# Sixteen groups of bins that end in two pairs, in place of fifteen that end in four threes

## The chip, the cores and the metric

The kernel runs on one core of a Trainium2 chip. The metric is the device time of one execution in microseconds. An execution under the profiler is slower than a timed one, and the two are kept apart below.

## The reference

A graph layer is followed by a mixture of eight experts, over 6,250 nodes with 256 features and 100,000 edges that are sorted by target:

```
x = x + GNN(layernorm(x)):  agg = segment_sum(xn[dst], src);  h = agg + xn
                            out = (h @ W1 + b1) @ W2 + b2
x = x + FFN(layernorm(x)):  for each of 8 experts: h1 = relu(bn(y @ W1)), h2 = relu(bn(h1 @ W2)), h2 @ Wo + bo
                            summed with the weights softmax(y @ Wr + br)
```

The sum over the edges is the sparse part. The experts are the dense part. Their matrices are 256x256, and each product is made as three half-precision passes (high x high, high x low, low x high).

## The kernel before

**Bins and entries.** The 6,250 nodes are 49 bins of 128. A prologue (the first 300 us of the profile) sorts the edges on the chip, makes the normalised and projected rows, writes them to memory (`xn_hilo`), and splits the weights. The edges then stand in 830 entries of up to 128 edges that all belong to one bin. 830 is fixed, as `BOUND`, whatever the edges are. GpSimd fetches each entry with one indirect DMA of 128 rows into `gbuf` (L544), a ring of 18 slots; before an even entry from the 18th on it waits until TensorE has used up the pair that held the slots. TensorE multiplies each entry by a one-hot matrix (L1504, L1505: two matmuls of 256 columns each, so four for a pair of entries). VectorE adds the result into the bin's row block `acc` (L1071) and makes the one-hot matrix of a later entry (L1002).

**Groups and steps.** The dense part goes through the bins in groups whose sizes are `GS`. A group of T bins takes eight steps, one for each expert. In step x TensorE issues, in this order:

- the first layer of step x+1, in two halves (L1, L1555): 6 matmuls each, 128\*T columns wide
- the third layer of step x-1 for the first two bins of the group (L3, L1589): 6 matmuls of 256 columns for each bin
- the second layer of step x, in two halves (L2, L1571), 6 matmuls each, 128\*T columns wide
- the third layer of step x-1 for bins three and four, if there are any

ScalarE makes, for each half of the first and the second layer, the rectified half-precision part (L730, L741) and the full one (L731, L742). VectorE subtracts the two to get the low part (L1167, L1173), and weighs the third layer into the output rows (L1190). The third layer of step x waits for the low parts of both halves of the second layer of step x.

**Where entries go.** `entry_plan` spreads the 415 pairs of entries over the steps. In steps 0 to 4 of group g the pairs that group g+1 needs are completed; from step 5 on the plan works for group g+2. The need of the first b bins is b/49 of the 830 entries. Thirteen pairs belong to the prologue. In a step the pairs stand at fixed places between the dense parts (`PLACES`). Entries and third layers share three PSUM banks in turn.

**Between groups.** In steps 3 to 7 of group g the next group's rows get their bias and aggregate, statistics, square root (L680), normalisation (L687), transposes (L1517), the logits of the router (L1527) and their exponentials (L716). SyncE loads a group's rows one group ahead and stores them when the last expert has been added (L459, L468).

Of the kernel before, what the change touches and what calls it, by code (L numbers as in the profile page):

```python
# [45 lines left out]
TILES = -(-E_EDGES // P)  # L46
BOUND = TILES + BINS - 1
GT = 4
GS = [1, 2, 3, 3] + [GT] * 7 + [3] * 4
G = len(GS)  # L50
FIRST = [sum(GS[:g]) for g in range(G + 1)]
NENT = BOUND
# [50 lines left out]
def nhalf(g):  # L103
    return 2 if GS[g] > 2 else 1

# [5 lines left out]
def bins_of(g, half):  # L111
    return range(2 * half, min(2 * half + 2, GS[g]))

# [30 lines left out]
def build(nc, x, src, dst, gW1, gb1, gW2, gb2, Wr, br, bn, W1, W2, Wo, bo, out):  # L144
    xn_dram = nc.dram_tensor("xn_hilo", (NPAD, 2 * D), F16, kind="Internal").ap()
    x_dram = nc.dram_tensor("x_whole_bins", (NPAD, D), F32, kind="Internal").ap()
    with ExitStack() as ctx:
# [160 lines left out]
        def loads_upto(g):  # L308

            return 16 * sum(GS[i] for i in range(g % 2, g + 1, 2))  # L310

# [84 lines left out]
        def _(sp):  # L396
# [56 lines left out]
            def load_x(g):  # L453
# [3 lines left out]
                    skip_runtime_bounds_check_because=IN_RANGE)  # L457
                for i in range(GS[g]):
                    sp.dma_start(xt[:, g % 2, i, :], x_dram[bass.ds(b[i] * P, P), :]).then_inc(s[f"xt_in{g % 2}"], 16)  # L459
# [1248 lines left out]
```

## Time and profile before

| | |
|---|---|
| timed runs | 1381.16, 1381.36, 1383.55 us, median 1381.36 |
| profiled execution | span 1595.0 us from the first to the last instruction; no other time of it is given |
| busy in the profile | PE 80%, VectorE 75%, ScalarE 54%, GpSimd 50% |
| mean granted TensorE clock | 0.928 of full speed |
| first and last indirect DMA issued | 235.8 and 1497.0 us |

The profiled execution takes 214 us more than a timed one. So a duration of a single instruction is taken from the profile, but the length of a stretch has to be looked through for idle time that the timed run may not have.

### The profile page before, as it was taken

To read this page: it belongs to the slowest core of one execution; us is meant where nothing else is said; L and a number is where in the kernel's file an instruction comes from. 1 tells how busy PE (TensorE), PEld (TensorE's weight loads), DVE (VectorE), ACT (ScalarE), POOL (GpSimd) and SP (SyncE) were. 2 spreads that over 40 slices of the span, in tenths; PEclk is the share of its full clock that TensorE was granted. 3 is DMA by queue.
4 is the path that set the end of the run, shared out by engine and by line. 5 is a ranking of instruction groups with operands and counts; after the bars stand their busy time and mean duration, and the time that the engine had idled before them with its cause. 6 is when DMAs were issued, how large, how long until landed. Compare 5 with 4: busy or idle time off the path is not lost.

```text
span 1595.0 us, 25908 instructions
## 1 busy us (share of the span) xinstructions
PE 1279.8 (80%) x8179; PEld 841.9 (53%) x8179; DVE 1197.4 (75%) x3476; ACT 868.3 (54%) x1623; POOL 805.0 (50%) x864
## 2 busy tenths in 40 slices
PE   3868885557687778888878878898888998788998
PEld 3746652345454445455545545554555666565665
DVE  9999985566667666777777877777778887777865
ACT  7887451344455435454445544555545665555685
POOL 3000006666556666666666666666666556656300
PEclk9969997778799988999999999999999999999999
DMA  9301135333232332333333333343333323332200
GB/s 292 99 0 53 54 100 170 109 98 103 83 103 86 110 91 87 111 88 100 102 89 113 87 90 113 87 116 87 89 111 88 107 83 107 88 105 86 74 11 11
DMA packets 82235, 150.86 MB, mean 95 GB/s; under 512 B 16855, under 2 KB 55034, under 8 KB 82100
## 3 DMA queue, kind: packets, MB, share of 16 engines
q0 software_dynamic: 39840, 108.84, 23.8%
q1 hardware_dynamic: 42260, 40.36, 8.0%
q8 instruction: 67, 1.10, 0.3%
q14 instruction: 68, 0.56, 0.1%
HBM read 129.87 MB, written 19.27 MB: 94 GB/s over the span
## 4 chain that ended last, share of the span: by engine, by line
PE 47%; DVE 24%; issue 12%; another core or an unknown queue 8%; ACT 7%; DVEq 2%; ACTq 0%
PE PA L1555 11%; PE PB L1571 11%; DVE acc L1071 5%; PE PL L1589 4%; DVE zz L837 4%; PE PT L1589 4%; PE PN L1589 3%; DVE zz L838 3%; DVE onehot L1002 2%; DVE xt L1190 2%; ACT PB L742 2%; PE PN L1505 2%; PE PT L1505 1%; PE PT L1504 1%
## 5 line engine op out<-in xcount | busy, mean ns | idle before, releaser
L544 POOL DMA_INDIRECT gbuf<-xn_hilo,dsti x830 | 790.3, 952 | 667.5 <-issue 196.8
L741 ACT ACTIVATE h<-PB,bnt,bns 128x512 f16<-128x512 f32 (+3 forms) x240 | 167.7, 699 | 325.9 <-remote 177.5
L1555 PE MATMUL PA<-yT,wsplit 128*128 128x512 f16 (+3 forms) x1440 | 318.1, 361 | 13.0 <-issue 9.4
L1571 PE MATMUL PB<-h,wsplit 128*128 128x512 f16 (+3 forms) x1440 | 300.3, 347 | 5.6 <-issue 5.6
L730 ACT ACTIVATE h<-PA,bnt,bns 128x512 f16<-128x512 f32 (+3 forms) x240 | 167.8, 699 | 215.8 <-remote 104.2
L1555 PEld LDWEIGHTS PA<-yT,wsplit 128*128 128x128 f16 x1440 | 143.3, 103 | 114.9 <-issue 31.3
L1173 DVE TENSOR_TENSOR h<-PB,h 128x512 f16<-128x512 f32 (+3 forms) x240 | 139.9, 587 | 84.8 <-ACT PB L742 64.5
L1571 PEld LDWEIGHTS PB<-h,wsplit 128*128 128x128 f16 x1440 | 141.2, 101 | 98.3 <-issue 13.0
L1002 DVE TENSOR_SCALAR onehot<-iota_row,srel 128x128 f16<-128x128 f16 x830 | 178.2, 267 | 0.0
L1167 DVE TENSOR_TENSOR h<-PA,h 128x512 f16<-128x512 f32 (+3 forms) x240 | 139.5, 587 | 40.2 <-ACT PA L731 31.8
L1071 DVE TENSOR_TENSOR acc<-acc,PN 128x256 f32 x276 | 114.0, 413 | 71.9 <-issue 23.8
L731 ACT ACTIVATE PA<-PA,bnt,bns 128x512 f32<-128x512 f32 (+3 forms) x240 | 160.8, 670 | 0.0
L742 ACT ACTIVATE PB<-PB,bnt,bns 128x512 f32<-128x512 f32 (+3 forms) x240 | 160.6, 669 | 0.0
L1071 DVE TENSOR_TENSOR acc<-acc,PT 128x256 f32 x286 | 118.0, 413 | 46.5 <-remote 16.1
L1071 DVE TENSOR_TENSOR acc<-acc,PL 128x256 f32 x268 | 110.6, 413 | 51.6 <-remote 21.1
L1589 PE MATMUL PN<-wsplit,h 128*128 128x256 f16 x792 | 104.9, 281 | 24.2 <-DVE xt L1190 7.2
L1589 PE MATMUL PL<-wsplit,h 128*128 128x256 f16 x828 | 107.6, 278 | 18.9 <-DVE acc L1071 6.3
L1589 PE MATMUL PT<-wsplit,h 128*128 128x256 f16 x732 | 96.1, 280 | 14.9 <-DVE acc L1071 7.2
L1589 PEld LDWEIGHTS PN<-wsplit,h 128*128 128x128 f16 x792 | 77.6, 100 | 50.1 <-issue 32.5
L1589 PEld LDWEIGHTS PL<-wsplit,h 128*128 128x128 f16 x828 | 80.1, 99 | 45.1 <-issue 24.7
L1504 PE MATMUL PN<-gbuf,onehot 128*128 128x256 f16 x276 | 72.2, 286 | 36.8 <-issue 28.8
L1504 PE MATMUL PL<-gbuf,onehot 128*128 128x256 f16 x268 | 70.7, 287 | 35.5 <-issue 30.6
(250 smaller groups left out, 1856.5 us busy)
## 6 DMA issues: line engine op xcount, KB each, us to landing
gbuf<-xn_hilo,dsti POOLq DMA_INDIRECT x830
xt<-x_whole_bins SPq DMA_DIRECT2D x49, 128.0 KB
out<-xt SPq DMA_DIRECT2D x49, 128.0 KB
acc<-in_x SPq DMA_DIRECT2D x4, 1536.0 KB
x_whole_bins<-acc SPq DMA_DIRECT2D x4, 1536.0 KB, 11.8
xn_hilo<-xt SPq DMA_DIRECT2D x24, 256.0 KB, 2.1
h<-in_L_ffn_W SPq DMA_DIRECT2D x9, 256.0 KB, 4.3
zz<-in_L_ffn_W SPq DMA_DIRECT2D x5, 256.0 KB
```

Source lines behind the costliest of these rows:

```text
L544: pool.indirect_dma_start(gbuf[:, k % SLOTS, :], None, xn_dram, bass.IndirectOffsetOnAxis(dsti[:, k:k + 1], 0)).then_inc(gat[k % SLOTS], 16)
L730: nc.scalar.activation(h1[:, e % 2, 0, h, 0:w], PA[:, h, 0:w], ACT.Relu, bias=sh, scale=sc)
L731: nc.scalar.activation(PA[:, h, 0:w], PA[:, h, 0:w], ACT.Relu, bias=sh, scale=sc).then_inc(s["z1_ready"], 1)
L741: nc.scalar.activation(h2[:, e % 2, 0, h, 0:w], PB[:, h, 0:w], ACT.Relu, bias=sh, scale=sc)
L742: nc.scalar.activation(PB[:, h, 0:w], PB[:, h, 0:w], ACT.Relu, bias=sh, scale=sc).then_inc(s["z2_ready"], 1)
L1002: ins = V.tensor_scalar(onehot[:, k % SLOTS, :], iota_row[:], srel[:, k:k + 1], None, ALU.is_equal)
L1071: V.tensor_tensor(to, to, bank(("E", p))[:, i, :], ALU.add).then_inc(s["acc_done"], 1)
L1173: V.tensor_tensor(h2[:, e % 2, 1, h, 0:w], PB[:, h, 0:w], h2[:, e % 2, 0, h, 0:w], ALU.subtract).then_inc(s["lo2_ready"], 1)
L1504: T_.matmul(to[:, i, :], onehot[:, m, :], gbuf[:, m, 0:D], start=True, stop=False)
L1555: last = T_.matmul(PA[:, h, 0:w], wsp[0][:, e, k, wp, h * P:(h + 1) * P], yT[:, g % 2, yp, k, 0:w], start=n == 0, stop=n == 5)
L1571: last = T_.matmul(PB[:, h, 0:w], wsp[1][:, e, k, wp, h * P:(h + 1) * P], h1[:, e % 2, yp, k, 0:w], start=n == 0, stop=n == 5)
L1589: last = T_.matmul(to[:, i % 2, :], h2[:, e % 2, yp, k, i * P:(i + 1) * P], wsp[2][:, e, k, wp, :], start=n == 0, stop=n == 5)
```

## The change

One line of sizes. A group of four goes, and the last of the four groups of three is followed by two groups of two:

```diff
-GS = [1, 2, 3, 3] + [GT] * 7 + [3] * 4
+GS = [1, 2, 3, 3] + [GT] * 6 + [3] * 4 + [2] * 2
```

Both lists sum to 49 bins. Everything else follows from `GS`: the number of groups, the widths of the matmuls and activations, the registers that address the bins, and the plan of the entries.

## Rows read from the trace of the kernel before

**Rows 1.** The page, engines: busy time, share of the span, instructions.

```profile
PE 1279.8 (80%) x8179; PEld 841.9 (53%) x8179; DVE 1197.4 (75%) x3476; ACT 868.3 (54%) x1623; POOL 805.0 (50%) x864
```

**Rows 2.** Windows, groups 0, 8, 10, 13, 14: length, busy PE PEld DVE ACT POOL, clock, DMA, GB/s.

```profile
301.10:373.00 71.90, 45.03 (x371) 34.25 (x370) 45.57 (x166) 34.43 (x85) 46.12 (x48) 0.80 0.37 108
...
1050.10:1152.90 102.80, 86.51 (x564) 51.69 (x565) 77.16 (x238) 52.06 (x83) 64.72 (x69) 0.98 0.34 98
...
1246.40:1327.00 80.60, 78.32 (x532) 50.37 (x529) 65.21 (x196) 50.14 (x80) 48.10 (x51) 0.98 0.32 94
...
1484.20:1544.00 59.80, 55.91 (x420) 38.89 (x418) 44.76 (x126) 43.74 (x80) 9.36 (x10) 1.00 0.13 36
1544.00:1595.00 51.00, 43.01 (x310) 29.54 (x307) 28.60 (x67) 32.64 (x57) 0.00 (x0) 0.98 0.05 16
```

**Rows 3.** Windows of line L742 alone: length, busy time and count, clock, DMA.

```profile
1050.10:1152.90 102.80, 11.94 (x16) 0.98 0.34 98
```

**Rows 4.** Waits of GpSimd: in total, times, longest.

```profile
POOL gbuf L544 <- issue: 196.8, 641, 0.7
```

**Rows 5.** Timeline of GpSimd, the first and the last gather: start, duration, idle before.

```profile
235.82 1.19 POOL L544 DMA_INDIRECT gbuf<-xn_hilo,dsti  x1 [195.71 <-DVE dsti L1012]
```

```profile
1496.96 0.94 POOL L544 DMA_INDIRECT gbuf<-xn_hilo,dsti  x1 [0.31 <-issue]
```

**Rows 6.** Timeline, a stall in group 12.

```profile
1444.18 0.67 ACT L741 ACTIVATE h<-PB,bnt,bns 128x384 f16<-128x384 f32 x1 [4.18 <-remote]
```

**Rows 7.** Timeline of PE in group 10, four bins: a half layer and what follows it.

```profile
1277.64 1.46 PE L1555 MATMUL PA<-yT,wsplit 128*128 128x512 f16 x6
1278.94 0.27 PE L1504 MATMUL PN<-gbuf,onehot 128*128 128x256 f16 x1
```

**Rows 8.** The chain of waits in group 14, one step: start, length, what.

```profile
1564.28 1.95 PE PA L1555 x12
1566.23 1.31 PE PT L1589 x12
1567.54 1.95 PE PB L1571 x12
1569.49 0.65 PE PN L1589 x6
```

**Rows 9.** Timeline of the last two steps of group 14, where no first layer is left.

```profile
1583.31 1.47 PE L1589 MATMUL PT<-wsplit,h 128*128 128x256 f16 x12 [1.43 <-ACT PB L742]
...
1584.61 2.11 PE L1571 MATMUL PB<-h,wsplit 128*128 128x384 f16 x12
...
1585.79 0.67 ACT L741 ACTIVATE h<-PB,bnt,bns 128x384 f16<-128x384 f32 x1 [3.17 <-PE PB L1571]
...
1586.92 0.67 ACT L741 ACTIVATE h<-PB,bnt,bns 128x384 f16<-128x384 f32 x1
...
1587.47 0.65 ACT L742 ACTIVATE PB<-PB,bnt,bns 128x384 f32<-128x384 f32 x1
1588.15 0.56 DVE L1173 TENSOR_TENSOR h<-PB,h 128x384 f16<-128x384 f32 x1 [0.57 <-ACT PB L742]
...
1588.81 1.47 PE L1589 MATMUL PL<-wsplit,h 128*128 128x256 f16 x12 [1.43 <-ACT PB L742]
```

**Rows 10.** Timeline of group 1, two bins: ScalarE and PE.

```profile
390.88 0.56 ACT L741 ACTIVATE h<-PB,bnt,bns 128x256 f16<-128x256 f32 x1 [5.36 <-remote]
391.34 0.53 ACT L742 ACTIVATE PB<-PB,bnt,bns 128x256 f32<-128x256 f32 x1
...
391.79 0.56 ACT L741 ACTIVATE h<-PB,bnt,bns 128x256 f16<-128x256 f32 x1
...
396.84 0.82 PE L1571 MATMUL PB<-h,wsplit 128*128 128x256 f16 x6
```

**Rows 11.** Groups by line and shape: count, busy us, mean ns, idle before.

```profile
L742 ACT ACTIVATE PB<-PB,bnt,bns 128x256 f32<-128x256 f32 x16 | 8.6, 537 | 0.0
...
L1173 DVE TENSOR_TENSOR h<-PB,h 128x256 f16<-128x256 f32 x16 | 6.4, 416 | 1.5 <-ACT PB L742 1.5
```

## The prediction

> **What bounds the kernel now.** I read the page first. TensorE is busy for 80% of the span, but no engine is full [rows 1], and the profiled span of 1595.0 us is 214 us over the timed 1381.4. So I cut the dense part into its fifteen groups. The cuts are where ScalarE begins the second layer of a group's first step; a group holds 16 instructions of L742 [rows 3]. Then I asked which resource each group's length follows [rows 2].
>
> Group 10 (four bins, 25 pairs of entries) takes 80.6 us with PE busy for 78.3 of it: it is bound by TensorE. Group 8 (four bins, 34 pairs) takes 102.8 us with PE busy for only 86.5, and holds 68 gathers (a 69th is cut by the border), which is 1.51 us for each. The gap comes from stalls in which ScalarE, VectorE and GpSimd all wait for results of TensorE that the trace shows as finished some us before [rows 6]. They come in nearly every group with gathers, and hardly in groups 10 and 14. I take them as the profiler's share, for this reason: a gather that waits for nothing is busy 0.95 us and then 0.31 us idle "issue" (196.8 us in 641 times) [rows 4], so 1.26 us. From the first gather at 235.8, 830 of them at 1.26 end at 1281.6; behind the last gather the profile has another 98.0 us, to 1595.0 [rows 5]. That makes 1379.6, against 1381.4 timed. So the timed run is at the pace of GpSimd's gathers almost to the end of the gathers, without the stalls.
>
> TensorE stands close behind. A half layer of 512 columns takes 1.30 us for 6 matmuls [rows 7], 0.217 each, a third layer 0.109 for each matmul of 256 columns [rows 8], so a pair of entries (four such) takes 0.44. Group 10 with 34 pairs in place of 25 would take 80.6 + 9 x 0.44 = 84.6 us of TensorE; its gathers would take 68 x 1.26 = 85.7. Four-bin groups in the middle are thus balanced, gathers ahead by one us. Group 13 (three bins, 15 pairs) takes 59.8 us, and group 14 (three bins, no entries) 51.0. A three-bin step in group 14 is TensorE alone: 1.95 + 1.31 + 1.95 + 0.65 = 5.86 us [rows 8].
>
> **The change, part by part.** The plan's arithmetic gives the pairs of each group. Groups 0 to 7 stay as they are. From there:
>
> - before, from group 8: 4 bins/34 pairs, 4/31, 4/25, 3/26, 3/25, 3/15, 3/0
> - after, from group 8: 4/31, 4/25, 3/26, 3/25, 3/22, 3/17, 2/10, 2/0
>
> So four groups are the same, only earlier. What goes is 4/34, 3/15 and 3/0. What comes is 3/22, 3/17, 2/10 and 2/0.
>
> *What goes.* 4/34: 85.7 us by its gathers (84.6 by TensorE; 102.8 as profiled, the far bound). 3/15: eight steps of 5.86 are 46.9, 15 pairs are 6.6, together 53.5; the group took 59.8, so 6.3 us belong to the work for the next group and to a stall of some 2 us. I take 5.5 for that work (bounds 4.4 and 6.3), so 59.0. 3/0: 51.0. In all 195.7 us.
>
> *3/22 and 3/17.* 46.9 + 22 x 0.44 + 5.5 = 62.1, and 46.9 + 17 x 0.44 + 5.5 = 59.9. Their gathers take 55.4 and 42.8 us, less than that, so they are hidden behind TensorE. This is 122.0 us.
>
> *A two-bin step.* TensorE's columns for a bin are the same in any group. The 6 matmuls of a half layer with 256 columns span 0.82 us with the last one's modelled 0.27 [rows 10], so 0.11 each: half the price of 512 columns. A step costs TensorE 36 x 0.109 = 3.93 us. The split costs the columns nothing. [...]
>
> But a two-bin step is too short for its own chain. The third layer of step x needs the low part of the second half of layer two, and stands ahead of layer two of step x+1 in TensorE's queue. The last steps of group 14 show this loop with nothing else in it [rows 9]: third layer at 1583.31, second layer at 1584.61 (1.30), ScalarE at 1585.79 (1.18), its second half at 1586.92 (1.13), the full part at 1587.47 (0.55), VectorE at 1588.15 (0.68), the next third layer at 1588.81 (0.66). The loop is 5.50 us, under TensorE's 5.86, so it costs nothing at three bins. At two bins: 1.31 for 12 matmuls as before; 6 x 0.109 + 0.2 = 0.86 to ScalarE; 0.91 for its half (390.88 to 391.79) and 0.46 to the full part [rows 10]; that takes 0.54, then 0.04 to VectorE; its subtraction 0.42 [rows 11] and 0.10 to TensorE. Sum 4.64 us, against TensorE's 3.93. ScalarE's load of four such halves is 3.65, so it is not the bound itself. Bounds for the step are 3.93 (the loop does not bind) and 5.2 (clock, below); I take 4.64, since every part has its row. With two pairs in a step TensorE has 3.93 + 0.87 = 4.80 and becomes the bound again; the entries fill the gap that the loop leaves.
>
> *2/10 and 2/0.* 2/10: five steps of 4.80, three of 4.64, and the work for the next group. That was 5.5 for three bins; most of it is in single instructions (table loads, square root, statistics) that do not shrink with the bins, so 4.5 (bounds 3 and 6): 42.4 us. 2/0: group 14 took 51.0, of which 46.9 are steps; its last two ran at 5.50, so 4.8 us stand outside; one bin less in the last third layer, weighing and store takes 0.9 off. 8 x 4.64 + 3.9 = 41.0. Together 83.4 us.
>
> *Edits at no cost.* SyncE's loads and stores stay 49 each; the load for the last group waits for a store of the group before, and has two steps (9 us) before its rows are wanted. GpSimd's 830 gathers are the same. Their ring gives a lead of at most nine pairs, which the last four-bin group, bound by TensorE, fills in both kernels.
>
> *Sum.* 122.0 + 83.4 - 195.7 = +9.7 us. On the timed median: 1391. A little of the lower clock that group 0 shows (0.80) can come back in groups with gaps in every step, so I say 1392.
>
> **The rivals.**
>
> *The loop does not bind (no change).* If layers one of later steps and the activations slip past each other so that a two-bin step costs 3.93, the eleven steps without entries save 0.71 each, 7.8 in all: +1.9 us, 1383. For it: group 14 runs without a gap at three bins. Against it: the loop of 5.50 is seen, and the order on TensorE is fixed. 14%.
>
> *The gathers bind to the end (faster).* What the kernel does after its last gather shrinks. Before, 98.0 us follow it. After, the last gather is let go when pair 406 is used up, in the first step of 2/10, and some 84 us follow. If the groups before ran at the gathers' pace the time would be 14 us less: 1367. In the profiled execution, at 1.51 us for each gather, 3/22 would take 66 us and be bound by them. This decides once the timed gather costs more than 62.1 / 44 = 1.41 us; but then 830 gathers alone would put the kernel before at 1504. It could hold in part, if the removed four-bin group costs well over 85.7 in the timed run: from 98 us on the change is a gain. 12%.
>
> *The clock falls in the two-bin groups (slower still).* [...] At 0.80 the TensorE part of the loop (2.17 us) takes 2.7, and steps with entries 4.80 / 0.80 = 6.0: 11 x 0.54 + 5 x 1.2 = 12 us more, 1403. The gaps in a two-bin step are 0.7 us each, where group 0's gaps are of several us (a stall of 4 to 5 us each [rows 6, 10]); that speaks against it. [...] 15%.
>
> **How the numbers follow.** The forecast has 59%, the rivals 14, 12 and 15. About 0.2%, 2.8 us, is what a measurement tells here from no change. The forecast and the clock rival are slower by more than that (74%; I say 72, for the price of the removed group is inferred), the second is within it (15%), the third faster (13%). The forecast's own bounds: the between-group work moves it by 1 to 3 us, the removed group by 1. The range runs from half of the way to the fast rival, 1374, to past the clock rival, 1407; most of the 12% and some slower cases stay out.
>
> **What would show it.** In the last group, successive activations of L741 of the same half 4.6 to 4.7 us apart, with PE idle about 0.7 us once a step, released by VectorE's low part; in group 14 4.8 to 4.9 us in steps with entries; matmuls of 256 columns 0.109 apart; two-bin groups of about 42 and 41 us; the last gather some 84 us before the end; a granted clock above 0.93 there. The profiled span hardly moves, to about 1590: its stalls make the removed group worth 102.8 us and 3/22 some 66, so 66 + 60 + 42 + 41 stand against 213.6. It is wrong if two-bin steps run at 3.9 us, if the clock there is at 0.8, or if the time falls although the tail is as forecast; then the four-bin group was dearer than its gathers.

## The result, and the profile after

The changed kernel takes 1393.48 us (median of 4 runs, 1392.50 to 1394.71), the kernel before 1381.91 beside it. The ratio is 1.0083, with a 95% interval of 1.0071 to 1.0095: 11.6 us slower. The forecast was 1392, slower.

The profiled execution of the changed kernel spans 1392.1 us, no more than a timed run. The stalls of [rows 6] are not in it. So I had the kernel before profiled a second time (below, `before_again`): 1380.5 us. That a profiled execution is slower than a timed one thus holds for the first profile alone. The comparison of profiles goes by these two. First the page of the changed kernel, then its windows: length, busy time of PE, PEld, VectorE, ScalarE and GpSimd, clock, DMA share, GB/s. The rows are groups 8 (4/31), 12 (3/22), 13 (3/17), 14 (2/10) and 15 (2/0), bins and pairs.

```profile
PE 1217.3 (87%) x8371; PEld 836.9 (60%) x8371; DVE 1196.0 (86%) x3519; ACT 895.8 (64%) x1691; POOL 810.8 (58%) x864
```

```profile
902.00:983.80 81.80, 79.71 (x546) 50.44 (x545) 72.80 (x224) 52.40 (x84) 61.99 (x66) 1.00 0.40 117
...
1187.70:1249.90 62.20, 59.46 (x455) 42.42 (x453) 54.58 (x176) 44.30 (x80) 42.40 (x45) 1.00 0.38 108
1249.90:1305.40 55.50, 55.19 (x432) 40.65 (x430) 48.02 (x152) 42.00 (x77) 32.17 (x34) 1.00 0.32 93
1305.40:1351.50 46.10, 40.93 (x356) 33.71 (x353) 31.16 (x93) 35.62 (x77) 0.00 (x0) 0.96 0.06 18
1351.50:1392.10 40.60, 29.00 (x251) 23.60 (x250) 20.50 (x56) 25.91 (x57) 0.00 (x0) 0.99 0.04 13
```

These answer to [rows 2]. In group 13 PE is busy for 55.2 of 55.5 us: nothing but TensorE counts. In group 15 it is busy for only 29.0 of 40.6 us: it waits for something once a step. The next lines, the timeline of group 15, say why; they answer to [rows 9].

```profile
1377.54 1.47 PE L1589 MATMUL PN<-wsplit,h 128*128 128x256 f16 x12 [0.54 <-ACT PB L742]
...
1378.85 1.47 PE L1571 MATMUL PB<-h,wsplit 128*128 128x256 f16 x12
...
1379.70 0.56 ACT L741 ACTIVATE h<-PB,bnt,bns 128x256 f16<-128x256 f32 x1 [0.90 <-PE PB L1571]
1380.17 0.53 ACT L742 ACTIVATE PB<-PB,bnt,bns 128x256 f32<-128x256 f32 x1
1380.62 0.56 ACT L741 ACTIVATE h<-PB,bnt,bns 128x256 f16<-128x256 f32 x1
...
1381.07 0.54 ACT L742 ACTIVATE PB<-PB,bnt,bns 128x256 f32<-128x256 f32 x1
1381.64 0.42 DVE L1173 TENSOR_TENSOR h<-PB,h 128x256 f16<-128x256 f32 x1 [0.49 <-ACT PB L742]
...
1382.17 1.47 PE L1589 MATMUL PL<-wsplit,h 128*128 128x256 f16 x12 [1.85 <-ACT PB L742]
```

From third layer to third layer (1377.54 to 1382.17) are 4.63 us: 1.31 to layer two, 0.85 to ScalarE, 0.92 to its second half, 0.45 to the full part of that, 0.57 to VectorE and 0.53 to the next third layer. Each engine waits for the one before. PE is idle ahead of each round: 0.54 us ahead of the first one shown, 1.85 us ahead of the second, where no first layer is left to fill the time.

The last gather of the changed kernel, and what GpSimd waited for in the whole execution:

```profile
1304.30 0.94 POOL L544 DMA_INDIRECT gbuf<-xn_hilo,dsti  x1 [0.30 <-issue]
```

```profile
POOL gbuf L544 <- PE PN L1505: 16.3, 29, 2.8
POOL gbuf L544 <- PE PT L1505: 16.3, 26, 2.8
POOL gbuf L544 <- PE PL L1505: 13.3, 27, 2.0
```

It goes out 22.7 us later than in the second profile of the kernel before. GpSimd waits up to 2.8 us at a time for slots, where it waited at most 0.5 us in `before_again`: TensorE is behind.

### The profile page after: what moved, and what is told of

Its sections match the earlier page's. It is cut to its first block, busy times and chain, and to the rows that moved or that the text cites. A ratio compares the mean times of both kernels' runs of the same rounds, so it can differ in the third digit from the quotient of the medians.

```text
span 1392.1 us, 26447 instructions
## 1 busy us (share of the span) xinstructions
PE 1217.3 (87%) x8371; PEld 836.9 (60%) x8371; DVE 1196.0 (86%) x3519; ACT 895.8 (64%) x1691; POOL 810.8 (58%) x864
## 4 chain that ended last, share of the span: by engine, by line
PE 36%; POOL 24%; DVE 18%; issue 11%; DMA 6%; ACT 4%; DVEq 1%; ACTq 0%; POOLq 0%
POOL gbuf L544 24%; PE PB L1571 9%; PE PA L1555 8%; DMA gbuf<-xn_hilo,dsti 6%; DVE zz L837 5%; DVE zz L838 4%; PE PL L1589 4%; PE PT L1589 3%; PE PN L1589 3%; DVE acc L1071 2%; PE PT L1504 1%; DVE onehot L1002 1%; DVE xt L1190 1%; PE PT L1505 1%; PE PL L1504 1%
## 5 line engine op out<-in xcount | busy, mean ns | idle before, releaser
L1555 PE MATMUL PA<-yT,wsplit 128*128 128x384 f16 (+3 forms) x1536 | 298.1, 332 | 3.9 <-DVE wsplit L1198 2.6
L741 ACT ACTIVATE h<-PB,bnt,bns 128x384 f16<-128x384 f32 (+3 forms) x256 | 173.1, 676 | 190.0 <-PE PB L1571 188.9
L1571 PE MATMUL PB<-h,wsplit 128*128 128x384 f16 (+3 forms) x1536 | 293.8, 331 | 0.0
L730 ACT ACTIVATE h<-PA,bnt,bns 128x384 f16<-128x384 f32 (+3 forms) x256 | 173.0, 676 | 167.4 <-PE PA L1555 166.2
L1173 DVE TENSOR_TENSOR h<-PB,h 128x384 f16<-128x384 f32 (+3 forms) x256 | 142.6, 560 | 49.6 <-ACT PB L742 48.6
L742 ACT ACTIVATE PB<-PB,bnt,bns 128x384 f32<-128x384 f32 (+3 forms) x256 | 164.8, 644 | 0.0
L731 ACT ACTIVATE PA<-PA,bnt,bns 128x384 f32<-128x384 f32 (+3 forms) x256 | 164.8, 644 | 0.0
L1167 DVE TENSOR_TENSOR h<-PA,h 128x384 f16<-128x384 f32 (+3 forms) x256 | 141.2, 558 | 19.3 <-ACT PA L731 18.1
L1071 DVE TENSOR_TENSOR acc<-acc,PN 128x256 f32 x290 | 119.7, 413 | 32.7 <-PE PN L1505 18.4
L1071 DVE TENSOR_TENSOR acc<-acc,PT 128x256 f32 x284 | 117.3, 413 | 29.8 <-PE PT L1505 14.9
L1071 DVE TENSOR_TENSOR acc<-acc,PL 128x256 f32 x256 | 105.7, 413 | 31.1 <-PE PL L1505 21.0
L1589 PE MATMUL PL<-wsplit,h 128*128 128x256 f16 x900 | 113.4, 274 | 5.6 <-ACT PB L742 2.4
L1589 PEld LDWEIGHTS PL<-wsplit,h 128*128 128x128 f16 x900 | 87.8, 98 | 26.2 <-issue 5.6
L1589 PE MATMUL PT<-wsplit,h 128*128 128x256 f16 x768 | 95.4, 273 | 4.1 <-ACT PB L742 2.4
L1504 PE MATMUL PT<-gbuf,onehot 128*128 128x256 f16 x284 | 73.1, 278 | 22.2 <-DMA gbuf<-xn_hilo,dsti 17.2
L1589 PE MATMUL PN<-wsplit,h 128*128 128x256 f16 x684 | 87.1, 275 | 4.4 <-issue 1.7
```

The costliest lines, as they stand in the source:

```text
L730: nc.scalar.activation(h1[:, e % 2, 0, h, 0:w], PA[:, h, 0:w], ACT.Relu, bias=sh, scale=sc)
L731: nc.scalar.activation(PA[:, h, 0:w], PA[:, h, 0:w], ACT.Relu, bias=sh, scale=sc).then_inc(s["z1_ready"], 1)
L741: nc.scalar.activation(h2[:, e % 2, 0, h, 0:w], PB[:, h, 0:w], ACT.Relu, bias=sh, scale=sc)
L742: nc.scalar.activation(PB[:, h, 0:w], PB[:, h, 0:w], ACT.Relu, bias=sh, scale=sc).then_inc(s["z2_ready"], 1)
L1071: V.tensor_tensor(to, to, bank(("E", p))[:, i, :], ALU.add).then_inc(s["acc_done"], 1)
L1173: V.tensor_tensor(h2[:, e % 2, 1, h, 0:w], PB[:, h, 0:w], h2[:, e % 2, 0, h, 0:w], ALU.subtract).then_inc(s["lo2_ready"], 1)
```

## The experiments

Edits of `GS` are shown against the changed kernel, ratios are to the kernel before.

**before_again: the kernel before, profiled once more.** No edit.

> The kernel before, unchanged, for a second profile. My theory (the stalls of the first profile are no part of a timed run; gathers at 1.26 us each set the pace up to the last one): a span near 1380 us, the four-bin group with 34 pairs near 85.7 us, the last gather near 1282 us, 98 us behind it. Rival (the stalls belong to the kernel): the span is again near 1595 us and that group near 102 us.

Measured: one timed run of 1382.28 us, span 1380.5. Its windows of groups 8 (4/34), 10 (4/25), 13 (3/15) and 14 (3/0), and its last gather:

```profile
901.20:985.60 84.40, 81.33 (x561) 52.08 (x560) 76.61 (x240) 52.55 (x83) 63.69 (x69) 1.00 0.41 118
...
1066.70:1140.70 74.00, 74.00 (x517) 48.77 (x516) 65.56 (x198) 50.70 (x80) 56.03 (x60) 1.00 0.41 118
...
1269.10:1329.70 60.60, 58.18 (x429) 40.73 (x428) 45.12 (x126) 44.18 (x81) 10.35 (x11) 0.97 0.14 40
1329.70:1380.50 50.80, 42.80 (x308) 29.33 (x305) 28.38 (x67) 32.39 (x57) 0.00 (x0) 1.00 0.05 16
```

```profile
1281.55 0.95 POOL L544 DMA_INDIRECT gbuf<-xn_hilo,dsti  x1 [0.30 <-issue]
```

The stalls were not there again: they were the first profile's own. The gathers keep their pace to the last one at 1281.55, and 98.9 us follow.

**swap: the third layer out of the loop.** On the changed kernel:

```diff
+                swap = halves_of(x) == 1
+                if swap:
+                    L2(x, 0)
                 if x:
                     L3(x - 1, 0)
-                L2(x, 0)
+                if not swap:
+                    L2(x, 0)
```

> The changed kernel, but in groups of one or two bins TensorE does the first half of layer two ahead of the third layer of the step before, so the third layer leaves the loop. My theory (the loop sets a two-bin step at 4.63 us): the step falls to TensorE's 3.93 us, 11 steps without entries save 0.7 each, 8 us in all, 1386 us, ratio to before 1.003. Rival (a two-bin step is dear through fixed costs of its instructions, whatever their order): no change, 1393 us, ratio 1.008.

Measured: 1386.64 us, ratio to the kernel before 1.0028 (1.0016 to 1.0040). The two groups of two, and the middle of the last one:

```profile
1306.80:1349.20 42.40, 38.47 (x356) 33.30 (x353) 31.12 (x92) 35.95 (x76) 0.00 (x0) 1.00 0.07 21
1349.20:1386.00 36.80, 28.41 (x251) 23.90 (x250) 20.35 (x56) 26.23 (x57) 0.00 (x0) 0.99 0.05 15
```

```profile
1365.03 1.47 PE L1589 MATMUL PL<-wsplit,h 128*128 128x256 f16 x12
...
1368.95 1.47 PE L1589 MATMUL PT<-wsplit,h 128*128 128x256 f16 x12
...
1372.88 1.47 PE L1589 MATMUL PN<-wsplit,h 128*128 128x256 f16 x12
```

The third layers now start 3.92 and 3.93 us apart, and no wait stands before them. The groups fall from 46.1 and 40.6 to 42.4 and 36.8 us. The edit also acts on groups 0 and 1, of one and two bins, which together take what they took (122.3 against 122.4 us). Timed, the new order takes away 6.8 of the 11.6 us (1393.48 - 1386.64), and 7.5 by the windows; 1.7 of these 7.5 are not the loop but a stretch of lower clock in group 14 of the changed kernel (below, `quarter_after`). The same instructions of the same sizes take less in another order, so their fixed costs were not it.

**four_last: one group of four in place of the two twos.**

```diff
-GS = [1, 2, 3, 3] + [GT] * 6 + [3] * 4 + [2] * 2
+GS = [1, 2, 3, 3] + [GT] * 6 + [3] * 4 + [GT]
```

> Fifteen groups, the four that the change removes put at the end as one group of four: sizes 1 2 3 3, six 4, four 3, one 4. My theory (sum over the groups of the larger of TensorE's and the gathers' time): 3/29 and 3/20 and 4/0 take 65.6 (TensorE; the lead of nine pairs covers its gathers) + 61.7 + 67.4 = 194.7 us in place of 195.7 for what goes, so 1381 us, between 1379 and 1387, ratio 0.998 to 1.004. Rival (what follows the last gather sets the time): the last gather goes out in step 2 of the last but one group, and 5 steps of it and a group of four, some 108 us, follow in place of 98: 1391 us, ratio 1.007.

Measured: 1386.32 us, ratio 1.0036 (1.0022 to 1.0050). Groups 12 (3/29), 13 (3/20) and 14 (4/0), and its last gather:

```profile
1185.50:1251.70 66.20, 63.26 (x488) 45.32 (x487) 62.06 (x208) 44.74 (x80) 50.05 (x54) 1.00 0.41 117
1251.70:1319.40 67.70, 62.51 (x449) 42.08 (x448) 51.16 (x147) 46.20 (x84) 24.87 (x26) 0.97 0.24 67
1319.40:1383.70 64.30, 57.02 (x362) 34.56 (x360) 35.78 (x76) 38.35 (x57) 0.00 (x0) 0.98 0.05 15
```

```profile
1283.24 0.95 POOL L544 DMA_INDIRECT gbuf<-xn_hilo,dsti  x1 [0.30 <-issue]
```

The time is at the upper end of my range and 5 us short of the rival's 1391. 3/29 takes 66.2 us for a term of 65.6, 4/0 takes 64.3 for 67.4, and 3/20 takes 67.7 where I had 61.7. The gathers hold 3/20 for 1.0 us at most: their pace (1.26 us each, eight a step) would make 10.1 us of each of its five steps with four pairs, but these start 7.9 to 9.5 us apart, and TensorE's gaps in front of entries come to 1.0 us in that group. Its longest gap is one of 3.04 us, in front of the transposes for the next group, and at its end the granted clock falls to 0.50 for some 3 us. How the 6 us divide was not tried. The last gather is where it was and 100.5 us follow, not 108.

**threes: sizes 1 and sixteen 3.**

```diff
-GS = [1, 2, 3, 3] + [GT] * 6 + [3] * 4 + [2] * 2
+GS = [1] + [3] * 16
```

> Seventeen groups: one of 1 bin, sixteen of 3. My theory (loss comes where a group's bins and its entries do not match, as in the four-bin group with 25 pairs that takes 80.6 us of TensorE against 63 us of gathers): all groups have 25 or 26 pairs, TensorE 63.5 and gathers 64 us each, so the mismatch of some 20 us goes: 1361 us, ratio 0.985. Rival (each further group costs its fixed work between groups, some 5 us): two more groups than before, 1392 us, ratio 1.007.

Measured: 1367.53 us, ratio 0.9893 (0.9878 to 0.9908): faster than both kernels. Its last three groups (3/25, 3/15, 3/0) and last gather:

```profile
1192.10:1256.10 64.00, 61.16 (x468) 43.52 (x466) 57.74 (x189) 44.57 (x80) 48.44 (x52) 1.00 0.41 118
1256.10:1316.70 60.60, 58.17 (x430) 40.71 (x428) 45.12 (x126) 44.23 (x80) 18.69 (x20) 0.97 0.21 60
1316.70:1367.50 50.80, 42.82 (x308) 29.36 (x306) 28.40 (x67) 32.41 (x57) 0.00 (x0) 1.00 0.05 16
```

```profile
1279.64 0.94 POOL L544 DMA_INDIRECT gbuf<-xn_hilo,dsti  x1 [0.30 <-issue]
```

The last two groups are the same as those of the kernel before, to 0.1 us, and the last gather goes out only 1.9 us earlier. What is different is where TensorE stands. When 3/15 begins, the kernel before has 11 gathers in that window left and the threes have 20 (one of each is cut by the border). In the kernel before TensorE is nine gathers further behind, and group 10 is where such a backlog can grow (4/25: PE busy for all of its 74.0 us, its 50 gathers worth 63 at 1.26 us each). That backlog is worked off after the last gather: 98.9 us against 87.9. With the 1.9 us these 11.0 make up the difference of the spans, 13.0. That the backlog comes from groups whose bins and entries do not match is read from the windows and not tried by itself, and the list differs at its start too (1 3 3 in place of 1 2 3 3). The direction of my expectation held, the size (20 us) did not; 14.4 came. Two further groups cost nothing that shows.

**quarter_before and quarter_after: a quarter of the gathers left out.** The same edit on both kernels; the sums over the edges lack the right rows there:

```diff
+                if k >= SLOTS and (k // 2) % 4 == 3:
+                    continue
                 pool.indirect_dma_start(gbuf[:, k % SLOTS, :], None, xn_dram,
...
-                    pe.wait_ge(gat[m], 16 * (k // SLOTS + 1))
+                    if not (k >= SLOTS and (k // 2) % 4 == 3):
+                        pe.wait_ge(gat[m], 16 * fetched(k))
```

`fetched(k)` counts the gathers into that slot up to entry k.

> The kernel before with a quarter of the gathers left out: from the 19th entry on, every fourth pair is not fetched and multiplies what its slots held, so the sums over the edges are not the reference's. GpSimd's work falls from 830 x 1.26 to 627 x 1.26 us. My theory (gathers set the pace in groups 0 to 8, and TensorE is close behind): the groups fall to TensorE's time, most in groups 0 to 3; 40 to 60 us less, 1320 to 1340 us. Rival (TensorE sets the pace everywhere but in group 0): 20 us less or under.

> The changed kernel with the same quarter of the gathers left out. My theory (the added groups 3/22, 3/17, 2/10 and 2/0 are bound by TensorE and the loop, with their gathers hidden): these four groups take 204 us as before, and the distance to the kernel before with the same quarter left out is again 9 to 14 us. Rival (the change costs by its gathers, the last of which goes out 23 us later): without the pressure of the gathers the distance falls to under 5 us.

Measured: 1336.99 and 1351.31 us, ratios to the kernel before 0.9673 (0.9658 to 0.9688) and 0.9775 (0.9760 to 0.9789). Windows of groups 0 to 3 and 4 to 8, first of `before_again`, then of `quarter_before`:

```profile
279.30:561.60 282.30, 225.37 (x1759) 156.12 (x1757) 229.62 (x779) 164.84 (x325) 214.35 (x224) 0.98 0.40 117
561.60:985.60 424.00, 407.12 (x2791) 258.38 (x2790) 380.25 (x1181) 263.44 (x411) 321.03 (x339) 1.00 0.41 118
```

```profile
278.90:530.20 251.30, 218.43 (x1761) 161.15 (x1760) 224.72 (x776) 164.44 (x326) 167.40 (x174) 0.96 0.36 106
530.20:943.00 412.80, 402.48 (x2792) 260.84 (x2791) 379.81 (x1184) 262.99 (x412) 240.62 (x253) 1.00 0.33 94
```

The gathers cost 31.0 us in groups 0 to 3 and 11.2 in groups 4 to 8: they set the pace there, by far most where groups are small and grow. The last four groups of `quarter_after`:

```profile
1145.80:1208.00 62.20, 59.50 (x456) 42.39 (x454) 54.54 (x177) 44.35 (x81) 32.77 (x34) 1.00 0.29 84
1208.00:1263.40 55.40, 55.09 (x431) 40.52 (x430) 47.94 (x151) 41.90 (x76) 24.55 (x26) 1.00 0.25 75
1263.40:1307.80 44.40, 39.22 (x356) 32.90 (x353) 30.94 (x92) 35.49 (x76) 0.00 (x0) 1.00 0.07 20
1307.80:1348.40 40.60, 29.09 (x252) 23.60 (x250) 20.60 (x56) 25.99 (x57) 0.00 (x0) 0.98 0.04 13
```

They are the same with fewer gathers, but for 1.7 us in group 14. These 1.7 us are TensorE's clock. Below is TensorE in that group in the changed kernel, then the same third layer in `quarter_after` (L1589 is L1595 there), then the window of the slow stretch in the changed kernel:

```profile
1335.17 0.66 PE L1517 MATMUL PT<-ident,hs 128*128 128x128 f32 x4 [2.20 <-ACT hs L687]
...
1337.38 2.73 PE L1589 MATMUL PL<-wsplit,h 128*128 128x256 f16 x12
```

```profile
1295.02 1.47 PE L1595 MATMUL PL<-wsplit,h 128*128 128x256 f16 x12
```

```profile
1336.60:1339.90 3.30, 3.30 (x17) 2.28 (x16) 1.45 (x3) 1.90 (x4) 0.00 (x0) 0.50 0.00 0
```

After a gap of 2.20 us the granted clock fell to 0.50, and the twelve matmuls took 2.73 us. In `quarter_after` the gap is 2.21 us, the clock stays at 1.00 (1291.0 to 1298.5 us), and they take 1.47 us. The kernel before has such a stretch too, in 3/15, which takes 60.6 us, and 58.9 in `quarter_before`, where the clock is 1.00. So in the profiles the two about cancel.

The distance of the two kernels is 14.3 us, just past the expected 9 to 14 and not under 5. The change does not cost through the gathers; their lateness in it is a consequence.

**one_two: a single group of two at the end.**

```diff
-GS = [1, 2, 3, 3] + [GT] * 6 + [3] * 4 + [2] * 2
+GS = [1, 2, 3, 3] + [GT] * 8 + [3] * 2 + [2]
```

> Fifteen groups that end in one group of two: sizes 1 2 3 3, eight 4, two 3, one 2. 4/34, 3/22, 3/10 and 2/0 stand in place of 3/26, 3/25, 3/15 and 3/0. My theory: 84.4 + 62.2 + 56.3 + 40.6 = 243.5 in place of 64.7 + 63.6 + 60.6 + 50.8 = 239.7 us, +3.8: 1386 us, ratio 1.003; half of it is the loop in the two-bin steps and the rest the bins that meet too few entries. Rival (a shorter last group pays, and only the sixteenth group cost): 10 us less than before for the shorter last group, 1372 us.

Measured: 1387.06 us, ratio 1.0032 (1.0022 to 1.0043), 4.8 us over the kernel before beside it, where 3.8 were expected. A shorter last group does not pay.

**threes_twos: the threes, ending in three twos, with the edit of `swap`.**

```diff
-GS = [1, 2, 3, 3] + [GT] * 6 + [3] * 4 + [2] * 2
+GS = [1] + [3] * 14 + [2] * 3
```

> Eighteen groups: one of 1 bin, fourteen of 3, three of 2, with the third layer out of the loop in groups of one or two bins. My theory: against the kernel with sixteen threes (1367.5 us), 3/22, 3/17, 2/17, 2/10 and 2/0 take 62.1 + 55.5 + 45.5 + 42.4 + 36.8 = 242.3 us in place of 239.9: 1370 us, ratio 0.991. Rival (what follows the last gather alone sets the time, and it is shorter in twos): some 8 us less than the threes, 1360 us, ratio 0.984.

Measured: 1372.50 us, ratio 0.9931 (0.9918 to 0.9945), 5 us over the threes, where 2.4 were expected. Even with the loop removed, twos at the end do not pay.

## Why the prediction was right, point by point

**What bounds the kernel.** That the stalls were no part of a timed run, and that the gathers keep their pace up to the last one, is shown by the second profile: last gather at 1281.55 (the estimate was 1281.6), 98.9 us behind it (98.0). "Four-bin groups in the middle are balanced, gathers ahead by one us": 4/34 takes 84.4 us, and 83.2 in the window of that group when the gathers are no limit:

```profile
859.80:943.00 83.20, 80.81 (x562) 52.34 (x561) 76.47 (x240) 52.58 (x84) 47.65 (x51) 1.00 0.33 95
```

**The terms of the sum.**

| term | forecast, us | measured, us |
|---|---|---|
| 4/34 goes | 85.7 | 84.4 |
| 3/15 goes | 59.0 | 60.6 |
| 3/0 goes | 51.0 | 50.8 |
| 3/22 comes | 62.1 | 62.2 |
| 3/17 comes | 59.9 | 55.5 |
| 2/10 comes | 42.4 | 46.1 |
| 2/0 comes | 41.0 | 40.6 |
| sum | +9.7 | +8.6 |

Both 3/15 and 2/10 hold the stretch of lower clock shown above; without it 3/15 takes 58.9 us (the term was 59.0) and 2/10 takes 44.4. The two spans differ by 11.6 us, three more than the terms. The changed kernel reaches group 8 0.8 us later (902.0 against 901.2), which may be scatter. The other 2.2 are no scatter. "Four groups are the same, only earlier" cost them nothing in my sum, but they are a little longer. The windows of the four, first in `before_again` and in `quarter_before`, then in the changed kernel and in `quarter_after`:

```profile
985.60:1269.10 283.50, 276.47 (x2004) 187.45 (x2003) 254.56 (x798) 192.35 (x321) 214.64 (x226) 1.00 0.41 118
```

```profile
943.00:1225.80 282.80, 276.14 (x2004) 187.31 (x2003) 254.42 (x798) 192.21 (x321) 151.66 (x160) 1.00 0.30 88
```

```profile
902.00:1187.70 285.70, 277.37 (x2003) 187.11 (x2002) 254.71 (x800) 192.15 (x320) 215.45 (x226) 1.00 0.40 118
```

```profile
860.50:1145.80 285.30, 277.09 (x2003) 187.06 (x2002) 254.44 (x800) 192.16 (x320) 150.35 (x159) 1.00 0.30 88
```

Every column of work is equal to within 1 us, at the same clock, and the difference (2.2 and 2.5 us) is there with and without the pressure of the gathers. So it is a wait, not work and not the gathers. It goes with where the groups stand: in `four_last`, where the same four groups stand at the same places, they take 285.9 us. In the changed kernel these groups have the other parity (4/25 is group 9 in place of 10), and their pairs fall on other places of the three shared banks and of the loads of ten addresses that VectorE makes every fifth pair. Parity alone is not it: in `one_two` 4/25 is group 11, odd as in the changed kernel, and takes 74.0 us as in the kernel before, not 75.0. Which of the other two it is was not tried.

Two terms were mis-sized, and cancel. Group 3/17 runs at TensorE's pace with hardly a gap, 4.4 us under my term, in which I charged the full 5.5 us of between-group work though the next group is one of two bins. Some 1.3 us of the 4.4 are only a matter of the border: 24 matmuls of first layers in that window belong already to the next group and have 256 columns, not 384. What the forecast says of single instructions holds in part: in the windows of groups 12 (for three bins), 13 and 14 (for two) the two table loads take 1.28 us each and the square root 0.30 us, but the statistics (L1107) are one instruction of 0.41 to 0.43 us for each bin.

In 2/10 "the entries fill the gap that the loop leaves" did not hold: steps with two pairs took 4.9 to 6.5 us, not 4.80. TensorE had work to fill the gap, but VectorE adds one of the step's two pairs into `acc` (L1071) between the two low parts of layer two (L1173), so the entries lengthen the loop itself. The step of 5.89 us in the changed kernel, and the loads of addresses (duration ns min/median/max, first and last start):

```profile
1317.62 0.42 DVE L1173 TENSOR_TENSOR h<-PB,h 128x256 f16<-128x256 f32 x1 [0.53 <-ACT PB L742]
1317.96 0.54 ACT L742 ACTIVATE PB<-PB,bnt,bns 128x256 f32<-128x256 f32 x1
...
1318.91 0.97 DVE L1071 TENSOR_TENSOR acc<-acc,PT 128x256 f32 x2 [0.86 <-PE PN L1505]
...
1319.81 0.42 DVE L1173 TENSOR_TENSOR h<-PB,h 128x256 f16<-128x256 f32 x1
...
1320.32 1.47 PE L1589 MATMUL PL<-wsplit,h 128*128 128x256 f16 x12 [0.92 <-issue]
```

```profile
L1054 DVEq TENSOR_LOAD <-bofs x83: 1061/1068/1578, 246.6 to 1317.6; - x83
```

ScalarE has the second full part ready at 1318.50, but its low part begins at 1319.81, 1.3 us late, and 4.63 + 1.3 is the step of 5.9. VectorE's 0.86 us of idle time is the last load of ten addresses, which starts at 1317.6 and takes 1.06 us; the matmuls of the pair that it then adds had ended before, at 1317.65. In the next step, without a load, the low part is 0.3 us late and the step takes 4.93 us. No run moved the addition, so this is read from the trace alone. `swap` takes the third layer out of the loop and so of this wait too, and the group took 42.4 us, 2.0 less than the 44.4 at full clock.

**The two-bin step.** Forecast 4.64 us by the loop, measured 4.63, and 3.93 without it, as `swap` shows. The matmuls of 256 columns keep their 0.109 us: twelve of a second layer take 1.31 us in group 15 (1374.22 to 1375.53, start to start). Twelve of 512 columns take 2.59 us in the last group of `four_last` (1316.61 to 1319.20), 0.216 each. At these widths the time goes by the columns, and splitting a group of four costs them nothing.

**The rivals.** "The loop does not bind" is excluded by `swap`. "The gathers bind to the end" is excluded by the 55.19 us of PE in the 55.50 of group 13, and by the last gather, which came 22.7 us later; what followed it, 87.8 us, was near the 84 forecast. Its gain was eaten before it began. "The clock falls in the two-bin groups": 0.96 and 0.99, where I asked for 0.80 in that case. What fell is the one stretch in group 14 shown above, 1.7 us, behind a single gap of 2.20 us; the kernel before lost as much in 3/15. The small gaps of the loop went with no lower clock: from 1351.5 to 1391.0 us group 15 has gaps of 0.53 to 1.85 us ahead of its third layers and a granted clock of 1.00. The 1 us that the forecast adds for a lower clock (1391 to 1392) was the author's estimate from group 0 alone; the whole changed kernel has a mean of 0.970, `before_again` one of 0.969. The stalls of 4 to 5 us that the prediction names there for group 0 are rows of ScalarE in groups 12 and 1; TensorE's longest gap in group 0 of that profile is 5.3 us.

**What was wrong, and what was luck.** The profiled span: "hardly moves, to about 1590". It was 1392.1, since the stalls of the first profile did not return. The direction and the loop were right with their reasons. That the total came within 1.5 us was in part luck: 3/17 was 4.4 us too dear, 2/10 3.7 us too cheap, and the 3.0 us outside the terms were in no sum.

**Where the 11.6 us are.** Without the loop the timed runs are 6.8 us shorter (`swap`). By the windows of the last two groups it is 7.5 (86.7 to 79.2 us), and 5.8 without the 1.7 us of lower clock (85.0 to 79.2); whether the timed runs had that stretch is not on record. Without the loop the four groups that come (62.1 + 55.5 + 42.4 + 36.8 = 196.8 us in `swap`) cost 1.0 us more than the three that go (195.8), or 2.7 more when 3/15 too is taken at full clock: the exchange alone costs little, the sixteenth group with it. 2.2 are the longer groups 8 to 11, cause open, and under 1 lies before them. `four_last`, with no two-bin group and fifteen groups, fits: its last three take 198.2 us, 2.4 over those that go, groups 8 to 11 another 2.4 over, and it is 3.2 us over in span, 4.4 in the timed medians.

## What to carry to other kernels

Before making pieces smaller, add up the loop through all engines once for the small size: from three bins to two TensorE's work for a step fell from 5.86 to 3.93 us here, the loop only from 5.50 to 4.63. Below the size at which the busiest engine covers the loop a piece costs more than its share (4.63 us for a two-bin step in place of 3.93). Ask of every engine in the loop what else stands in its queue between two links: here an addition of entries lengthened it. If the loop binds, look at the order within the queue before the size: moving one independent block out of the loop gave back over half of the loss in the timed runs. And where a producer (here the gathers) and a consumer (the dense steps) run side by side, equal pieces that hold both in the ratio of their speeds (the sixteen threes, 14.4 us faster) did better than any shorter end that was tried.

## What the runs showed that I had not expected

The first profile of the kernel before spans 1595.0 us and the second 1380.5, with the same instructions (25,908). In the first, ScalarE waits up to 7.5 us for results of TensorE, and 68 gathers of group 8 come 1.51 us apart; in the second, 1.26. No timed run was near 1595. A profile that is well over the timed runs should be taken again before its idle times are read. What caused those stalls stays open.
